# Softmax division in a Flamingo-style kernel: spreading matmuls replaced by transposes around a token-major division

## What is computed

```python
probs = softmax(scores, axis=-1)                  # per row, head, query: over 256 keys
out = einsum('bhqk,bhkd->bhqd', probs, v)         # weighed values
out = out.transpose(0, 2, 1, 3).reshape(b, s, E)  # heads side by side
x = x + tanh(g[l]) * (out @ Wo.T + bo)            # "mix"
```

## Time and profile before

| | before |
|---|---|
| median of 3 runs | 1298.04 us (1297.67 to 1299.72) |
| the profiled execution's own time | 1300.65 us |
| its span, first to last instruction | 1298.9 us |
| PE busy | 987.6 us, 76% |
| DVE busy | 801.5 us, 62% |
| ACT busy | 495.5 us, 38% |
| POOL busy | 294.1 us, 23% |
| mean granted TensorE clock | 0.798 of full |

### The profile page before, as it was taken

One profiled execution on the slowest core, in us unless ns is written; L12 is line 12 of the kernel. 1 busy time (PEld: TensorE's weight loads), 2 busy tenths in 40 slices (PEclk: granted clock), 3 DMA queues, 4 the chain that ended last, 5 costly groups with the idle time before them and its releaser, 6 DMA issues.

```text
span 1298.9 us, 19087 instructions
## 1 busy us (share of the span) xinstructions
PE 987.6 (76%) x7252; PEld 632.9 (49%) x7252; DVE 801.5 (62%) x1841; ACT 495.5 (38%) x752; POOL 294.1 (23%) x308
## 2 busy tenths in 40 slices
PE   0676868779987889869786978987789586957654
PEld 0423445556664457445563444566357443734441
DVE  2799988865745744785748587755854663371323
ACT  1554534433321465254234555323253333223213
POOL 1602154434111023123122042314021301020000
PEclk9889789787888799788787779678679776766576
DMA  7000000000000000000000000000000000000000
GB/s 267 25 2 2 2 1 2 2 2 1 1 2 1 5 23 17 5 2 18 1 1 5 2 18 2 1 1 1 1 6 1 1 2 5 1 1 5 1 0 5
DMA packets 11724, 14.24 MB, mean 11 GB/s; under 512 B 1588, under 2 KB 10700, under 8 KB 11380
## 3 DMA queue, kind: packets, MB, share of 16 engines
q1 hardware_dynamic: 10772, 6.85, 1.8%
q10 hardware_dynamic: 864, 6.18, 1.2%
HBM read 11.54 MB, written 1.05 MB: 10 GB/s over the span
## 4 chain that ended last, share of the span: by engine, by line
PE 51%; DVE 33%; ACT 6%; issue 5%; POOL 1%; DMA 1%; SPq 1%; POOLq 0%; DVEq 0%; ACTq 0%
PE banks L970 38%; DVE nm_row L1387 9%; PE pv L970 8%; DVE probs L1406 3%; DVE qf_row L1417 3%; PE banks L721 3%; DVE st_row L1260 2%; DVE xn_row L1341 2%; ACT probs L928 2%; DVE mv_row L1262 1%; DVE wide L1476 1%; ACT qT_row L855 1%; PE banks L1023 1%; PE banks L1039 1%; ACT wide L950 1%
## 5 line engine op out<-in xcount | busy, mean ns | idle before, releaser
L1387 DVE TENSOR_REDUCE nm_row<-banks 128x4 f32<-128x1024 f32 (+1 forms) x192 | 207.8, 1127 | 44.9 <-PE banks L970 44.5
L928 ACT ACTIVATE probs<-banks 128x1024 f32<-128x1024 f32 (+1 forms) x144 | 126.1, 931 | 89.3 <-PE banks L970 88.6
L785 POOL TENSOR_TENSOR rstd_row<-rstd_row,neghalf 128x2 f32<-128x2 f32 x66 | 47.6, 722 | 482.6 <-DVE rstd_row L1336 379.1
L970 PE MATMUL banks<-kT_row,qT_row 48*128 48x256 bf16 (+2 forms) x896 | 122.6, 330 | 39.8 <-DVE nm_row L1387 30.9
L970 PE MATMUL banks<-qT_row,kT_row 50*128 50x256 bf16 (+2 forms) x896 | 115.3, 332 | 46.9 <-DVE probs L1406 15.4
L970 PE MATMUL pv<-probs,vpad 128*32 128x256 f32 (+1 forms) x1536 | 115.7, 429 | 16.6 <-ACT probs L923 8.8
L970 PE MATMUL banks<-wide,c 128*128 128x256 f32 x512 | 126.8, 403 | 0.0
L970 PEld LDWEIGHTS banks<-kT_row,qT_row 48*128 48x128 bf16 (+1 forms) x896 | 54.3, 117 | 116.6 <-issue 53.2
L970 PEld LDWEIGHTS banks<-wide,c 128*128 128x128 f32 x512 | 100.2, 201 | 18.0 <-issue 0.9
L970 PEld LDWEIGHTS banks<-qT_row,kT_row 50*128 50x128 bf16 (+1 forms) x896 | 59.7, 121 | 97.6 <-ACT probs L928 23.8
L1406 DVE TENSOR_TENSOR probs<-banks,biasT_row 128x1024 f32<-128x1024 f32 x64 | 75.6, 1218 | 19.4 <-PE banks L970 18.1
(11 more groups left out here) (216 smaller groups left out, 1604.1 us busy)
## 6 DMA issues: line engine op xcount, KB each, us to landing
c<-in_c ACTq DMA_DIRECT2D x1, 2500.0 KB, 12.5
wide<-in_mask SPq DMA_DIRECT2D x8, 256.0 KB, 2.9
qT_row<-mT_row SPq DMA_DIRECT2D x96, 4.0 KB
c<-in_c ACTq DMA_DIRECT2D x1, 1194.5 KB, 6.9
late<-in_late ACTq DMA_DIRECT2D x2, 512.0 KB, 15.9
xn_row<-in_ctx SPq DMA_DIRECT2D x8, 128.0 KB, 5.0
x_row<-in_x SPq DMA_DIRECT2D x8, 128.0 KB, 2.7
out<-x_row SPq DMA_DIRECT2D x8, 128.0 KB, 1.9
```

The costliest lines, as they stand in the source:

```text
L785: return pool.tensor_tensor(t, t, neghalf[:, 0:n], ALU.pow)
L928: act.activation(dst[:, :, 0:w], src[:, :, 0:w], ACT.Exp, scale=1.0 if l == 2 else HD ** -0.5).then_inc(sem["probs"], 1)
L970: return pe.matmul(dst, lhsT, rhs, start=start, stop=stop, **kw)
L1387: V.tensor_reduce(nm[b][:, t, :, 2 * jp:2 * jp + 2], ps[:, :, :, 0:kn], AX.X, ALU.max, negate=True).then_inc(sem["max"], 1)
```

## The change

The division is done with tokens on partitions, for all four sublayers:

- `o_flip`, PE: four float32 transposes of 128 x 128 turn `weighed_sb` into one bank `o_ps` (tokens on partitions, features and sums along the free axis).
- `o_flip`, DVE: a reciprocal of 32 sums per partition (8 in sublayer 2) out of that bank into `qr`, then products that read the bank and the reciprocals with a broadcast: two of 128 x 128 in the 16-head sublayers, one of 128 x 256 in sublayer 2. They go to `qf`.
- `o_turn`, a new step: two float32 transposes of `qf` into a bank `oT_ps` on PE, and an `evac` by ACT into `oT`.
- `mix` is as before, and now waits for ACT.

`spreads` goes, with its memset, its eight transfers and the wait for them. `COST` and `starts_after` have entries for the new steps, so all lists are planned anew.

```diff
-EARLY = 4 + 2 * LANES
+EARLY = 4
...
-        out += [("divide", l, row), ("o_flip", l, row), ("mix", l, row)]
+        out += [("divide", l, row), ("o_flip", l, row), ("o_turn", l, row), ("mix", l, row)]
...
-        "o_flip": [("PE", 1.03), ("DVE", 2.13)], ("o_flip", 2): [("DVE", 2.13)], "mix": [("PE", .5), ("DVE", .4)],
+        "o_flip": [("PE", .75), ("DVE", .8)], "o_turn": [("PE", .42), ("ACT", .27)], "mix": [("PE", .5), ("DVE", .4)],
...
-        "o_flip": [("oT_ps", "one", "oT")] if l != 2 else [],
+        "o_flip": [("o_ps", "one", "o_normed")], "o_turn": [("oT_ps", "one", "oT")],
...
-                sp.wait_ge(setup_zero, 1)
-                for j in range(2):
-                    for c in range(LANES):
-                        row, head = COLS * c + j * (HD + 1), LANES * j + c
-                        sp.dma_start(spreads[row:row + HD + 1, :], dram["spreads"][head * (HD + 1):(head + 1) * (HD + 1), 0:P]).then_inc(early_in, 16)
...
-                pool.memset(spreads[:, :], 0.0).then_inc(setup_zero, 1)
...
+                    if kind == "o_turn":
+                        evac(oT[b][:, :], "oT_ps", bank("oT_ps", s)[:, 0:SEQ], "oT")
...
-                    if kind == "o_flip" and l != 2:
-
+                    if kind == "o_flip":
                         pe.wait_ge(sem["sums"], at("sums", s))
+                        claim(pe, "o_ps", s)
+                        for t in range(NT):
+                            for g in range(2):
+                                n = 2 * t + g
+                                ins = pe.transpose(bank("o_ps", s)[:, n * P:(n + 1) * P], weighed_sb[b][:, g, t * P:(t + 1) * P], ident)
+                        ins.then_inc(sem["o_ps"], 1)
+                    if kind == "o_turn":
+                        pe.wait_ge(sem["o_normed"], at("o_normed", s))
                         claim(pe, "oT_ps", s)
-                        for i, n in enumerate(("o", "r")):
-                            a, w = SPREAD_COLS[n]
-                            for g in range(2):
-                                ins = mm(bank("oT_ps", s)[g * w:(g + 1) * w, i * SEQ:(i + 1) * SEQ], spreads[:, a:a + w],
-                                         weighed_sb[b][:, g, :])
+                        for t in range(NT):
+                            ins = pe.transpose(bank("oT_ps", s)[:, t * P:(t + 1) * P], qf[b][:, t, :], ident)
                         ins.then_inc(sem["oT_ps"], 1)
...
                     if kind == "o_flip":
-                        over = qf[b][:, :, :].rearrange("p t d -> p (t d)")
+                        dve.wait_ge(sem["o_ps"], at("o_ps", s))
+                        ps = bank("o_ps", s)
                         if l == 2:
-                            dve.wait_ge(sem["sums"], at("sums", s))
-                            num, den = weighed_sb[b][:, 0, :], weighed_sb[b][:, 1, :]
+                            four = ps[:, :].rearrange("p (t n c d) -> p t n c d", t=NT, n=2, c=MQ)
+                            over = qr[b][:, 0, 0:NT * MQ].rearrange("p (t c) -> p t c", t=NT)
+                            ch.link(V.reciprocal(over, four[:, :, 1, :, 0]))
+                            V.tensor_tensor(qf[b][:, :, :].rearrange("p t (c d) -> p t c d", c=MQ), four[:, :, 0, :, :],
+                                            over[:, :, :, None].to_broadcast([P, NT, MQ, MD]), ALU.mult).then_inc(sem["o_normed"], 1)
                         else:
-                            dve.wait_ge(sem["oT_ps"], at("oT_ps", s))
-                            ps = bank("oT_ps", s)
-                            num, den = ps[:, 0:SEQ], ps[:, SEQ:2 * SEQ]
-                        ch.link(V.reciprocal(over, den))
-                        V.tensor_tensor(oT[b][:, :], num, over, ALU.mult).then_inc(sem["oT"], 1)
+                            strips = ps[:, :].rearrange("p (n c w) -> p n c w", n=2 * NT, c=LANES)
+                            over = qr[b][:, 0, 0:NT * HEADS].rearrange("p (n c j) -> p n c j", n=2 * NT, c=LANES)
+                            dst = qf[b][:, :, :].rearrange("p t (g j c d) -> p (t g) j c d", g=2, j=2, c=LANES)
+                            ch.link(V.reciprocal(over, strips[:, :, :, HD:2 * HD + 2:HD + 1]))
+                            for j in range(2):
+                                n = j * (HD + 1)
+                                ins = V.tensor_tensor(dst[:, :, j, :, :], strips[:, :, :, n:n + HD],
+                                                      over[:, :, :, j, None].to_broadcast([P, 2 * NT, LANES, HD]), ALU.mult)
+                                if j == 0:
+                                    ch.mark(ins)
+                            ins.then_inc(sem["o_normed"], 1)
```

More of the change, by code:

```diff
@@ L208, in starts_after @@
                 "weigh": [(of("attend", l, 2 * (part or 0) + n), "POOL" if l == 1 else "ACT") for n in range(2)],
-                "o_flip": [(of("divide", l), "ACT")], "mix": [(of("o_flip", l), "DVE")],
+                "o_flip": [(of("divide", l), "ACT")], "o_turn": [(of("o_flip", l), "DVE")], "mix": [(of("o_turn", l), "ACT")],
                 "route": [(of("flip", 4 + l), "ACT")],
@@ L223, in starts_after @@
                 "norm": [(of("stats", l), "POOL")],
-                "o_flip": [(of("divide", l), "ACT")] if l == 2 else [],
                 "mix": [(of("plus", l), "POOL")],
@@ L304, in signals @@
                 "q_turn": ["q_ready"], "q_mid": ["q_rest"], "q_low": ["q_stack"],
-                "max": ["max"], "shift": ["shift"], "attend": ["biased"], "o_flip": ["oT"], "mix": ["x_mixed"],
+                "max": ["max"], "shift": ["shift"], "attend": ["biased"], "o_flip": ["o_normed"], "mix": ["x_mixed"],
                 "route": ["logits", "gate_in"] if l == 1 else ["logits", "onehot"], "gate": ["onehot"],
@@ L313, in signals @@
                 "shift_flip": ["shiftT"], "attend": ["probs"] + (["v_placed"] if wide and s[3:] == (0,) else []),
-                "divide": ["sums"], "route": ["gate_exp"], "choose": ["onehotT"] + (["u"] if l == 1 else []),
+                "divide": ["sums"], "o_turn": ["oT"], "route": ["gate_exp"], "choose": ["onehotT"] + (["u"] if l == 1 else []),
                 "inner": ["h0"], "again": ["h1"], "deep": ["ht"]}[kind]
@@ L457, in build @@
         small_parts = sb("small_parts", [3 * E, P + FF], BF16)
-        spreads = sb("spreads", [P, P])
         def W(name):
@@ L558, in build @@
         early_in = ctx.enter_context(nc.semaphore("early_in"))
-        setup_zero = ctx.enter_context(nc.semaphore("setup_zero"))
         setup_act = ctx.enter_context(nc.semaphore("setup_act"))
```

## The result

The changed kernel takes **1311.6 us** (median of 4 runs, 1308.37 to 1316.38) against 1297.86 us of the kernel before on the same chip: a ratio of 1.0107, 95% interval 1.0074 to 1.014. It is slower by 14 us, where 7 us faster was forecast, and lies outside the range of 1276 to 1307. The profiled execution took 1308.37 us, with a span of 1306.1 us and a mean granted clock of 0.797.

What follows compares the result with a forecast made beforehand. No engine was full, so the chain alternating between PE and DVE was taken as the bound. Sum -12.1, start -1.5, coming back +6.9 made -6.7 us, forecast 1291 us, range 1276 to 1307.

Steps and rivals of the forecast that it cites:

- the new order: Rival: all lists shift; six `max` steps behind row 5's last `mix` cost 6.8 us: 1298, no change; chance 0.13 (new order or hidden).
- The sum: Savings and added latency over 20 blocks on the chain, order held fixed: -12.1 us, before the start and what comes back.
- Prices of the instructions: Work per engine after the change: DVE busy near 760 us, PE near 995, ACT near 508.
- The short reciprocal: DVE's reciprocal of 32 numbers in the division: 0.35 us, from the rows; the skill's rule would give 0.16.
- the 20 blocks of the chain: Of 32 blocks, the 20 whose reciprocal lies on the chain that ended last; 11 go out to PE, nine to DVE.
- The 12 blocks off the chain: The remaining blocks, costed at nothing because other rows cover them; 15 us of DVE relief there pays only if cover goes.
- The start: ACT and DVE begin without waiting for eight small transfers: gain between 0 and 3.4 us, taken as 1.5.
- The trip's latency: Before `mix`, two transposes, a copy and two more handoffs between engines: 1.02 us at full clock.
- The relief pays everywhere: Rival: DVE's 41.8 us less work counts at 33/62, 22 us, plus the start's 1.5: 1274.5 us; chance 0.15.
- The trip meets an exponential: Rival: ACT's copy waits a whole exponential, trip 2.3 us instead of 1.02 on 11 blocks, 14 us: 1305; chance 0.17.
- The clock falls: Rival: transposes replacing matmuls lower PE's clock, six taking 1.78 us instead of 1.05, 15.6 us on the chain: 1307; chance 0.05.
- "faster" against "slower": Whole kernel's sign: faster 0.65, within 0.2% 0.13, slower 0.22; wrong if PE's `xT_row` waits from ACT outgrow DVE's shrinkage.

Runs made afterwards that it cites:

- after_hop: The changed kernel, instructions unchanged, with the planner's handoff after DVE at 0.15 us instead of 0.14; measured 0.9957 of the kernel before.

## Why the prediction was wrong

**The step that failed** is the one on the new order. The sum was made "with the order held fixed", and the forecast for a kernel with all lists planned anew was taken from it. The new order stood only as a rival, priced at 6.8 us from the one place at the end that I could read, with "Other places may go either way", at a chance of 0.13. Measured, the order costs +17 us (1.0107 against 0.9974), and orders of the same instructions lie up to 28 us apart. The changed kernel's own order makes PE wait 33 us more than the old one does for `xn_row`, `mp_row` and `stack` (86.8 against 54.1), steps that the sum did not contain. Both the price and the side were wrong: the rival ended at "no change", and no case ended beyond 1307.

By its steps:

- *Prices of the instructions*: right. DVE 757 us (forecast 760), PE 994.5 (995), ACT 507 (508).
- *The short reciprocal*: 0.351 us for 32 numbers (0.35). The Trainium skill ("VectorE: DVE Perf Modes", section "The TRN2 errata") would have it, as an estimate from its figure, at 0.16 us; the trace does not agree, and going by the rows was right.
- *The sum at the old order*: -6.7 us forecast, -3.4 measured (interval -5.3 to -1.4). Near, but with terms of another size. The relief was counted on the 20 blocks of the chain: 46 us of work over 32 blocks, of which 20/32 are 29 us; it is worth 33. The turn's and copy's 1.02 us were charged in full to the blocks that go out to PE, and partly elsewhere; in all 32 blocks they cost 30. The sentence "The 12 blocks off the chain I cost at nothing: other rows cover them" does not fit the turn, unless the 20 blocks paid half more than the 1.02 us each; for the relief 33 against 29 points the same way, less clearly. The two errors nearly cancel, which is luck. Start -2.5, reciprocals -33.4, turn and copy +30.2 make -5.7, against -3.4 measured in one. These prices come from different kernels and depend on one another: the reciprocals gave 33 us in one and 53 in another.
- *The start*: 1.9 us earlier at ACT, 2.5 us in time (1.5 forecast), with an interval that includes none.
- *The trip's latency* was charged as 1.02 us, and 0.2 more for the copy's wait on ACT. The copy's wait is 0.37 us on average in the changed kernel (median 0.04, one of 4.7). What the sum left out is the turn's wait in PE's list: 2.3 us on average from the products' end, the three of 14 to 15 us among them.
- *The relief pays everywhere*: right as a mechanism, at 0.72 us a microsecond of DVE work, against the 0.53 (33/62) used. It did not show since the trip pays everywhere too.
- *The trip meets an exponential*: not so. PE's waits for `xT_row` out of ACT are 15.8 us in 24 waits, the longest 1.6, and moving the copy off ACT makes it slower.
- *The clock falls*: the mean granted clock is 0.797 against 0.798, with 128 + 64 transposes more and the spreading matmuls gone; the changed kernel's four executions range from 0.787 to 0.798. The Trainium skill's rule ("TensorE: Matmul & The Clock Gate", section "Part 4: PE-mode transpose") that transposes don't count as activity would have let it fall; in the changed kernel's mean no such thing shows. At the old order the turns did go with a lower clock, 0.790 against 0.809, but the shorter reciprocal alone moved it by as much (0.798 to 0.817) with no transpose changed, so this does not single them out. Since PE idles as long with the turn as without, waiting is not the reason there either: at the old order this rival is not ruled out.
- *"faster" against "slower"*: the statement of what would make the forecast wrong named the wait for `xT_row` out of ACT growing. It grew by 8 us, while the one for `xT_row` out of DVE fell by 29. The loss came in waits that were not on the list, `xn_row`, `mp_row` and `stack`.

What stays open is why an order is good. The runs show that PE waits 35 us more than before for three kinds of untouched steps, that turns stand behind a 15 us step of another row, and that lists which differ almost only behind 896 us take 25 us of those waits away again. They do not show by what mark a good list could be told before it runs.

## What to carry to other kernels

Where an edit makes a planner write all lists anew, time it twice: once in its own order, once with the old order kept. Here the first gave +14 us, the second -3.4 us, and moving a constant by 10 ns gave -5.6 us, so that a verdict on the first alone is one on the draw; a forecast of such a change needs a range of at least a per cent to either side of its sum, and a version to keep is found by drawing several orders (the best here, the change planned with measured durations, is 1.2% faster than the kernel before). Draw orders for the old version too: one of those was 0.6% faster with no new instruction. And where no engine is full, do not cost blocks off the chain that ended last at nothing without a test: turn and copy cost 30 us in all, where the chain's 20 blocks at their computed latency make 20.

## What the runs showed of the hardware

PE's busy time is no constant of its instructions. With the same matmuls it was 987.6 us in the kernel before and 966.8 with shorter reciprocals on DVE, at a granted clock of 0.798 and 0.817. Of the 39 us by which the two spans differ, more than half (20.8) is PE running faster, not waiting less. It works the other way too: in the old order with the new division, long reciprocals instead of short ones took PE's idle time from 295 to 325 us, and its busy time from 1000.2 to 1019.6, at a clock of 0.790 and 0.781; the span grew by 49 us for 30 us of waiting. In these two pairs a microsecond of PE's waiting went with 1.6 to 2.2 us of time. It is no fixed price: between the changed kernel and `after_hop` 24.5 us of waiting go with 20.5 us of span, and the turn at the old order adds 33 us of span with no more waiting at all.
